# Convolution through band matrices, routing batch by batch with the sums on GpSimd, and experts chosen in two groups

## What is computed

```
z = layernorm(x)                                        # per token
top = 1 where the channel context is among the 76 largest of 128 positions, else 0
conv input, branch c (top) and s (1 - top): [max, mean] over the positions -> [B, 2, 512]
A = sigmoid(relu(batchnorm(conv1d(input, 2 channels, 7 taps))))       # one value per batch and channel
x = x + z * (top * A_c + (1 - top) * A_s)
f = layernorm(x)
p = softmax(f @ router_w.T + router_b)                  # 8 experts
w = the two largest p of a token, divided by their sum
x = x + 0.5 * sum over experts of w * (f @ A.T) @ Bm    # rank 16
```

## Time and profile before

| | |
|---|---|
| runs | 1105.84, 1101.44, 1104.09 us; median 1104.09 |
| the profiled execution | 1102.04 us, its span 1100.3 us |
| busy over the span | TensorE 999.7 us (91%), VectorE 706.1, ACT 515.7, GpSimd 469.3 |
| mean granted TensorE clock | 0.967 of full speed |

### The profile page before, as it was taken

The page is one execution under the profiler, slowest core; times in us unless marked ns, Lnnn a source line. Parts: engine busy times, 40 slices in busy tenths (PEclk is TensorE's granted clock), DMA queues, the critical chain, the costliest instruction groups (busy, mean ns, idle before and its releaser), DMA issues. The chain is left out here.

```text
span 1100.3 us, 18306 instructions
## 1 busy us (share of the span) xinstructions
PE 999.7 (91%) x6010; PEld 844.0 (77%) x6010; DVE 706.1 (64%) x1844; ACT 515.7 (47%) x1330; POOL 469.3 (43%) x362
## 2 busy tenths in 40 slices
PE   4999999999999999999999999999999999565465
PEld 3888888888888888888888888888878887333353
DVE  6566565656576767586555665665676575587384
ACT  3454444444444554445543543553555344167251
POOL 5554444444444545434444354353444352344200
PEclk9999999999999999999999999999999999799577
DMA  6433333323333323334232132222212220000002
GB/s 205 146 94 94 95 95 93 94 93 95 93 96 96 92 89 97 117 99 133 59 105 82 32 104 70 72 82 82 72 62 82 82 63 23 20 1 1 1 1 77
DMA packets 50412, 87.71 MB, mean 80 GB/s; under 512 B 6368, under 2 KB 15200, under 8 KB 50336
## 3 DMA queue, kind: packets, MB, share of 16 engines
q1 hardware_dynamic: 50336, 86.76, 25.5%
HBM read 84.64 MB, written 2.10 MB: 79 GB/s over the span
## 5 line engine op out<-in xcount | busy, mean ns | idle before, releaser
L540 POOL TENSOR_TENSOR wq_lo<-raw_q,wq_hi 128x512 fp32r<-128x512 f32 x64 | 82.8, 1293 | 263.6 <-DVE prob L1213 257.3
L1493 PE MATMUL pX<-wv_lo,cT_hi 128*128 128x256 f32 x512 | 149.3, 292 | 0.2 <-ACT q_sb L678 0.2
L1196 DVE TENSOR_TENSOR score<-pS,b_mask 128x512 f32<-128x512 f32 x64 | 44.2, 691 | 161.4 <-PE pS L1671 148.1
L802 ACT ACTIVATE prob<-score,neg_max 128x128 f32<-128x128 f32 x256 | 99.7, 391 | 97.2 <-DVE neg_max L1199 97.2
L1494 PE MATMUL pX<-wv_hi,cT_lo 128*128 128x256 f32 x512 | 144.0, 281 | 0.0
L1495 PE MATMUL pX<-wv_hi,cT_hi 128*128 128x256 f32 x512 | 144.0, 281 | 0.0
L540 POOL TENSOR_TENSOR wv_lo<-raw_v,wv_hi 128x1024 fp32r<-128x1024 f32 x32 | 77.6, 2425 | 124.9 <-ACT wv_hi L678 124.9
L678 ACT ACTIVATE v_sb<-pX 128x512 f32<-128x512 f32 x64 | 38.2, 597 | 163.2 <-PE pX L1495 163.2
L1493 PE MATMUL pX<-xT_lo,wq_hi 128*128 128x512 f32 x256 | 106.0, 414 | 6.1 <-POOL wq_lo L540 5.1
L1493 PE MATMUL oacc<-wo_lo,aT_hi 128*128 128x512 f32 x256 | 100.5, 393 | 5.1 <-DVE aT_lo L1191 3.8
L1493 PE MATMUL pX<-cT_lo,wk_hi 128*128 128x512 f32 x256 | 105.0, 410 | 0.0
(11 more groups left out here) (276 smaller groups left out, 2387.1 us busy)
## 6 DMA issues: line engine op xcount, KB each, us to landing
raw_k<-in_wk SPq DMA_DIRECT2D x64, 256.0 KB, 2.9
raw_q<-in_wq SPq DMA_DIRECT2D x64, 256.0 KB, 3.5
raw_v<-in_wv SPq DMA_DIRECT2D x32, 512.0 KB, 4.2
raw_o<-in_wo SPq DMA_DIRECT2D x64, 256.0 KB, 2.7
b_raw<-in_bias SPq DMA_DIRECT2D x64, 64.0 KB, 2.8
g_raw<-in_w_gate SPq DMA_DIRECT2D x16, 172.0 KB
g_raw<-in_w_up SPq DMA_DIRECT2D x16, 172.0 KB
f_raw<-in_w_down SPq DMA_DIRECT2D x4, 688.0 KB, 4.7
```

Source lines behind the costliest of these rows:

```text
L540: g.tensor_tensor(w_lo[c][:], w_raw[c][:], w_hi[c][:].bitcast(F32), ALU.subtract).then_inc(s_w_lo[c], 1)
L802: e = a.activation(prob[:, b, :], score[:, b, :], ACT.Exp, bias=neg_max[:, b:b + 1], accum_out=row_sum[:, b:b + 1])
L1196: v.tensor_tensor(score[:], pS[:].rearrange("p (b s) -> p b s", b=HB), b_mask[:], ALU.add).then_inc(s_scored, 1)
L1493: mm(dst, lh, rl, start=start, stop=False, skip_group_check=lint)
```

## The change

The taps are no longer multiplied into the statistics. In seven attention steps (20 to 23, 28 to 30) VectorE builds two band matrices of 128 x 384 from `diag` and the taps, and the convolution is three products for each of them. ACT scales the means as it sums. Scale and shift of batch norm go into the Tanh, and relu behind it; a one-element Exp follows the Tanh. The mean over the channels is taken out of `ra` once (at token tile 0 of the second half), so that the routed rows are transposed and multiplied without subtracting the mean, and the reciprocal deviation is put on as ACT copies `rh`. Routing goes batch by batch: VectorE makes product and statistics, GpSimd the sum and the power. The choice is made for batches 0 to 3 while 5 to 7 are still being routed, then for 4 to 7; it takes the largest of the logits rather than of the probabilities, and divides by the sum of the two chosen. The expert products of batches 0 to 3 stand between the routing of 5 to 7.

```diff
+CHOSEN = 2.0 ** 127
+        BAND_STEPS = (20, 21, 22, 23, 28, 29, 30)
+        l_bank = (pYb[:].bitcast(F32), pA[:, 512:1024])
...
@@ gpsimd, at the end @@
-            with pool.Fori(0, B // 2) as p:
-                rsqrt(rs1[:], ve1[:], p + HB + 6)
+            def routed_rstd(t):
+                pool.wait_ge(s_x3_var, t + 1)
+                g.tensor_tensor(rs3[:, t:t + 1], ve3[:, t:t + 1], neg_half[:, 0:1], ALU.pow).then_inc(s_x3_rstd, 1)
+            for t in range(B):
+                pool.wait_ge(s_zc, t + 1)
+                g.tensor_tensor(xr[:, t, :], zc[:, t % 2, :], xr[:, t, :], ALU.add).then_inc(s_x3, 1)
+                if t >= 1:
+                    routed_rstd(t - 1)
+            routed_rstd(B - 1)
@@ scalar, sums of the statistics @@
                             last = a.activation(sum_junk[:, br, lt, :], split[:, br, lt, :], ACT.Copy,
+                                                scale=1.0 / (CRUCIAL, REST)[br],
@@ scalar, behind the feed-forward layer @@
             act.wait_ge(s_zn, 1)
-            a.activation(cz[:], cz2[:], ACT.Tanh, scale=0.5).then_inc(s_sig, 1)
+            for br in range(2):
+                last = a.activation(cz2[:, :, br, :], cz[:, :, br, :], ACT.Tanh, scale=bn_scale[:, br:br + 1],
+                                    bias=bn_shift[:, 0:1])
+            last.then_inc(s_sig, 1)
+            a.activation(exp_again[:], ident[:, 0:1], ACT.Exp)
             act.wait_ge(s_dA, 1)
...
+            def routed_heads(t):
+                act.wait_ge(s_r_proj, t + 1)
+                act.wait_ge(s_x3_rstd, t + 1)
+                a.activation(rh[:, t, :], pA[:, 0:E + ER], ACT.Copy,
+                             scale=rs3[:, t:t + 1]).then_inc(s_rh, 1)
...
+            weights_of(1)
+            weights_of(2)
+            for t in range(B):
+                routed_out(t)
+                if t + 3 < B:
+                    weights_of(t + 3)
+                if t == HB:
+                    route_exp(0)
+                if t > HB:
+                    lora_out(t - HB - 1)
+                routed_heads(t)
+            lora_out(HB - 1)
+            route_exp(1)
+            for t in range(HB, B):
+                lora_out(t)
@@ vector, in attention, called in step behind early_end @@
+            def bands(n):
...
+                    for c in range(2):
+                        tap = taps[:, c * TAPS + j:c * TAPS + j + 1]
+                        if j == 0:
+                            v.tensor_scalar(band[c][:], diag[:, 0:3 * P], tap, None, ALU.mult)
+                        else:
+                            last = v.scalar_tensor_tensor(out=band[c][:], in0=diag[:, j:j + 3 * P], scalar=tap,
+                                                          in1=band[c][:], op0=ALU.mult, op1=ALU.add)
@@ vector, behind attention @@
             for t in range(HB + 2):
+                if t == 0:
+                    dve.wait_ge(s_ra_sum, 1)
+                    v.tensor_scalar(ra_mean[:, 0, :], ra_bank, 1.0 / D, None, ALU.mult)
+                    dve.drain()
+                    v.tensor_tensor(ra[:], ra[:], ra_mean[:].to_broadcast([P, KT, E + ER]),
+                                    ALU.subtract).then_inc(s_ra, 1)
                 ffn_step(t)
-            for j in range(TAPS):
-                v.tensor_scalar(tapped[:, j], stat[0][:], taps[:, j:j + 1], None, ALU.mult)
...
             dve.wait_ge(s_conv, 1)
-            v.tensor_copy(cz[:], conv)
...
             dve.wait_ge(s_rstd, HB + 6)
+            v.tensor_scalar(bn_scale[:], rs1[:], gb[:, 0:1], 0.5, ALU.mult, ALU.mult).then_inc(s_zn, 1)
+            dve.wait_ge(s_sig, 1)
+            v.tensor_scalar(cz[:], cz2[:], 0.0, 0.5, ALU.max, ALU.mult)
             dve.drain()
+            v.tensor_scalar(other[:], cz[:, :, 1, :], 0.5, None, ALU.add)
+            v.tensor_tensor(dA[:], cz[:, :, 0, :], cz[:, :, 1, :], ALU.subtract).then_inc(s_dA, 1)
...
+            def gated(t):
+                dve.wait_ge(s_c_trans, t + 1)
+                if t >= 2:
+                    dve.wait_ge(s_x3, t - 1)
+                v.tensor_tensor(zc[:, t % 2, :], c_bank[t % 2][:], z[:, t, :], ALU.mult).then_inc(s_zc, 1)
+            def routed_stats(t):
+                dve.wait_ge(s_x3, t + 1)
+                v.bn_stats(st3[:, t, :], xr[:, t, :])
...
+                v.tensor_scalar(ve3[:, t:t + 1], mv3[:, t, 1:2], EPS, None, ALU.add).then_inc(s_x3_var, 1)
+            def route(i):
+                group = slice(i * HB, (i + 1) * HB)
+                dve.wait_ge(s_rh, (i + 1) * HB)
+                v.tensor_tensor(prb[:, group, 0:E], rh[:, group, 0:E], rb[:].to_broadcast([P, HB, E]), ALU.add)
+                for t in range(i * HB, (i + 1) * HB):
+                    v.max(best[:, t, :], prb[:, t, :])
+                v.tensor_tensor(logit[:, group, :], prb[:, group, 0:E],
+                                best[:, group, 0:1].to_broadcast([P, HB, E]), ALU.subtract).then_inc(s_top_logit, 1)
+                for t in range(i * HB, (i + 1) * HB):
+                    v.match_replace(prw[:, t, :], best[:, t, :], prb[:, t, :], CHOSEN)
+                dve.wait_ge(s_r_exp, i + 1)
...
+            gated(0)
+            gated(1)
+            for t in range(HB):
+                routed_stats(t)
+                gated(t + 2)
+            routed_stats(4)
+            route(0)
+            for t in range(HB):
+                weighed(t)
+            gated(6)
+            routed_stats(5)
+            finished(0)
+            gated(7)
+            routed_stats(6)
+            finished(1)
+            routed_stats(7)
+            finished(2)
+            finished(3)
+            route(1)
+            for t in range(HB, B):
+                weighed(t)
+            for t in range(HB, B):
+                finished(t)
@@ tensor @@
             for t in range(-1, HB + 2):
                 ffn_step(t)
+                if t == -1:
+                    pe.wait_ge(s_const_in, 16 * 6)
+                    for kt in range(KT):
+                        last = mm(ra_bank, ones[:], ra[:, kt, :], start=kt == 0, stop=kt == KT - 1)
+                    last.then_inc(s_ra_sum, 1)
...
+            for c in range(2):
+                pe.wait_ge(ready[c][0], EARLY_Z)
+                pe.wait_ge(ready[c][1], B - EARLY_Z)
+                mm(pA[:, 0:KT * width], band[c][:, P:2 * P], stat[c][:], start=c == 0, stop=False,
+                   skip_group_check=True)
+                mm(pA[:, width:KT * width], band[c][:, 2 * P:3 * P], stat[c][:, 0:KT - 1], start=False, stop=False,
+                   skip_group_check=True)
+                last = mm(pA[:, 0:(KT - 1) * width], band[c][:, 0:P], stat[c][:, 1:KT], start=False, stop=c == 1,
+                          skip_group_check=True)
...
+            coef_transposes(0)
+            coef_transposes(1)
+            for t in range(HB):
+                routed_transposes(t)
+                coef_transposes(t + 2)
+                router(t)
+            routed_transposes(4)
+            coef_transposes(6)
+            router(4)
+            routed_transposes(5)
+            hidden_transpose(0)
+            router(5)
+            coef_transposes(7)
+            hidden_transpose(1)
+            lora(0)
+            routed_transposes(6)
+            router(6)
+            hidden_transpose(2)
+            lora(1)
+            routed_transposes(7)
+            hidden_transpose(3)
+            lora(2)
+            router(7)
+            lora(3)
...
```

More of the change, by code:

```diff
@@ L129, in layers_kernel @@
         e_down = sbuf("e_down", [P, D])
+        stat = [sbuf(f"stat{c}", [P, KT, 2, B]) for c in range(2)]
         att = ExitStack()
@@ L921, in _ @@
             act.wait_ge(s_zn, 1)
-            a.activation(cz[:], cz2[:], ACT.Tanh, scale=0.5).then_inc(s_sig, 1)
-            act.wait_ge(s_dA, 1)
[L925 to L930, removed]
-                        last = a.activation(coef[:, t, lt, :], top[:, t // HB, lt, t % HB, :], ACT.Identity,
-                                            scale=dA[:, lt, at(t)], bias=cz[:, lt, 1, at(t)])
-                    last.then_inc(s_coef, 1)
@@ new lines, in _, with weights_of, routed_out @@
+            last.then_inc(s_sig, 1)
+            a.activation(exp_again[:], ident[:, 0:1], ACT.Exp)
+            act.wait_ge(s_dA, 1)
+            def weights_of(t):
+                for lt in range(KT):
+                    last = a.activation(coef[:, t, lt, :], top[:, t // HB, lt, t % HB, :], ACT.Identity,
+                                        scale=dA[:, lt, t:t + 1], bias=other[:, lt, t:t + 1])
+                last.then_inc(s_coef, 1)
+            def routed_out(t):
+                act.wait_ge(s_f_t, t + 1)
+                if t >= 2:
+                    act.wait_ge(s_r_proj, t - 1)
+                copy(fT[:, t % 2, :], f_bank[:, t % 2 * 512:(t % 2 + 1) * 512]).then_inc(s_fT, 1)
@@ L1868, in _, with coef_transposes @@
[L1868 to L1871 removed]
+            def coef_transposes(t):
+                if t == 0:
```

(24 more changed lines are left out.)

247 lines of the change are left out of this document (85 added, 162 removed).

## The result

The changed kernel takes 1086.7 us (median of four runs, 1084.2 to 1087.9) against 1102.97 in runs beside it: a ratio of 0.9853, 95% interval 0.9829 to 0.9878, 16.3 us faster. Two executions on record stand far apart from the others of their kernel and are in none of the ratios here: 1124.38 us of the kernel before, beside the first experiments, and 2038.98 us of the kernel with one choice. The changed kernel's profiled execution took 1084.23 us with a span of 1082.5, that of before 1102.04 with 1100.3.

What follows compares the result with a forecast made beforehand. TensorE bounds the kernel to about 945 us, handovers between engines the last 70 us. 6.85 + 0.2 + 2.4 + 0.7 + 3.8 − 0.1 = 13.9 us gives execution 1088.1, or 1090.2 as median; it took 1089, range 1083 to 1095.

Steps and rivals of the forecast that it cites:

- Bands in attention: Two VectorE instructions in each of seven attention steps, mostly in idle time: cost 0.1 us, bounds 0 and 0.4.
- attention ends within 0.5 us of before: Sign that the prediction is right: the end of attention moves by no more than 0.5 us.
- Mean of the router weights: Four TensorE products and two VectorE instructions before token tile 0 of the second half: costed at nothing, 1 us if uncovered.
- Convolution: Six products instead of 13, first batch-norm reduction straight from PSUM at 1034.0: gain 6.85 us, bounds 6.0 and 7.3.
- Batch norm and gates: From the reduction to the gate difference: smaller scaling, two Tanh, two more small VectorE instructions: gain 0.2 us.
- Routing: Gate difference to last row: ACT bounds at 2.5 to 2.8 us a batch, first choice delays products 6, 7: gain 2.4.
- Second choice: Last row to first weighted product: four batches, no table load, but VectorE waits 1.9 for output tile 3: gain 0.7.
- End: First weighted product to the span's end: four tiles at half clock, 1.7 us each, 11.3 in all: gain 3.8.
- full-clock rival: TensorE's clock stays high to the end or rises sooner, last four tiles take 0.97 each: gain 17.5, 1085.5; chance 0.2.
- contention: GpSimd and VectorE hold each other up in routing: 3 to 5 us, so 1092 to 1094; chance 0.16, late clock included.
- the batches don't overlap: Routing queues stand behind GpSimd's sum; wholly serial 7.1 us a batch, 12 us slower than before, 1115; chance 0.04.
- the clock never rises: All routing rows at half clock, 4.2 us of TensorE a batch, so the time is 1103; chance 0.05.

Runs made afterwards that it cites:

- the first experiments: The earliest follow-up runs, which the text doesn't single out; the kernel before had medians of 1102.3 to 1102.6 us beside the experiments.
- the kernel with one choice: Changed kernel with one choice of all eight batches behind the last row, all eight output tiles behind it: 1087.2 us.
- with it alone: Kernel before with only the new convolution (band matrices, means scaled on ScalarE, six products): 1097.4 us, ratio 0.9954.
- the filler: Changed kernel plus 20 unread bf16 products on TensorE behind output tile 3, while it waits for the second choice: 1085.0 us.
- the kernel with one choice and filler at the gates too: Changed kernel with one choice of all eight batches, unread TensorE products during it, ahead of the convolution, between batch-norm sums and during gates: 1083.2 us.
- that without the gate filler: Changed kernel with one choice of all eight batches and 21 unread TensorE products while it is made: 1082.9 us.
- no early Exp: Changed kernel without the one-element Exp behind Tanh, so the first choice loads the Exp table: 1090.7 us.
- the kernel without the hole: Changed kernel with product 6 and statistics 5 inside the first choice, output tile 3 finished behind the second choice's weighed products: 1085.3 us.
- the kernel with sums on VectorE: Changed kernel with the eight routing sums on VectorE behind each product, GpSimd keeping only the powers: 1089.2 us.
- the one with filler at the gates: Changed kernel plus unread TensorE products ahead of the convolution (10), between batch-norm sums (2) and during the gates (9): 1085.7 us.

## Why the prediction was right

It said 1089.0, range 1083 to 1095, 13.9 us gained in the span. It was 16.24 in the tail; the median of 1086.7 lies in the range. Of the gain 2.3 us were missed: the pace of the routing and the end were both costed too dear, by 2.8 together, and three small misses the other way come to 0.5.

- *Bands in attention*, costed 0.1: measured 0.2 to 0.3, of the seven steps. The sign "attention ends within 0.5 us of before" failed (1.25 sooner), but it could tell nothing of the bands, since that mark differs by more between executions. *Mean of the router weights*, costed at nothing: its subtraction took 1.20, and still ended ahead of SiLU's product; from attention's residual to the last split it is 82.8 before and 82.5 after.
- *Convolution*, 6.85: measured 6.78, and 6.70 with it alone. The sequence predicted is what the timeline shows.
- *Batch norm and gates*, 0.2: measured 0.03. The two Tanh take 0.72 together where 0.56 was taken.
- *Routing*, 2.4: measured 3.73. The mechanism was right (ScalarE sets the pace, a hole of 4 us before product 6), and the size off: "2.5 to 2.8 us a batch" should have been 2.31. The durations 0.60, 1.64 and 0.36 of neighbouring ScalarE instructions overlap by about 0.1 each; from start to start they are 0.50, 1.53 and 0.28. Adding durations and a handover for each overstated the busy engine's queue. The end of row 3 came 0.85 sooner behind dA than laid out (15.85 for 16.7), and the hole and what follows it gave another 0.4 (VectorE was held for 4.10 us, 1053.78 to 1057.88, for 4.5).
- *Second choice*, 0.7: measured 0.41; VectorE did wait for output tile 3, for 2.37 behind row 7 where 1.9 was taken.
- *End*, 3.8: measured 5.29. "Four tiles at half clock" held for one tile and part of the next; then the clock rose. Before, it had stayed low for two tiles and part of the third. From the first weighed product to the first tile's matmul it was 1.14, not 0.9. The full-clock rival stood 3.6 below the forecast, of which its own terms (four tiles at 0.97 for 1.7, two transposes at half their 0.2) give 3.1; 1.5 came by itself (9.77 for 11.3), and the filler brought another 1.46.

The mechanisms were right in each part. What the sum didn't show is which part of the routing and choice earns the gain. The one-choice kernel does: the new routing 8.5 (hardly for the clock: before, the sums of the last three pairs start 6.49 apart, at 1056.90, 1063.39 and 1069.88, with the clock low for the first and up for the second), the table load behind Tanh and the new choice 1.5, the two groups about nothing. They are neither good nor bad in themselves; they hold products 6 and 7 for as long as they hide tiles.

The rivals: contention is refuted (684 against 694 ns); "the batches don't overlap" and "the clock never rises" did not occur (rows 2.31 apart; 1.00 from 1046 to 1072); "the clock stays high to the end" was half true, for two of four tiles.

Attention's end differs by up to 4 us between executions, the largest disturbance in these medians (the kernel with one choice and filler at the gates too has a tail 2.1 shorter than that without the gate filler, and the same median). The traces show where most of it lies: in the granted clock, at two places. From the last score addition to the residual it takes 12.1 us in seven profiles, with the clock at 1.00, but 13.5 in four and 15.1 in one (no early Exp), in which the clock is at 0.50 for part of attention's last products. And in four profiles the clock falls at 724 to 726, behind an idle stretch of 1.95 us that the others have too, and that step takes 1.2 us longer. Busy time by stretch, the kernel with one choice, then the changed kernel, in the same output products:

```profile
944.00:946.00 2.00, 1.88 (x5) 1.50 (x6) 0.08 (x2) 0.00 (x0) 0.00 (x0) 0.50 0.00 0
...
942.00:944.00 2.00, 2.00 (x10) 1.63 (x10) 0.00 (x0) 0.00 (x0) 0.00 (x0) 1.00 0.00 0
```

Left open: why the clock falls there in some executions and not in others, with the same instructions.

## What to carry to other kernels

In a tail of small handovers, an idle stretch on TensorE costs twice: once as a wait, and again in the products behind it if the clock falls. A choice that was 1.4 us later went with a loss of 3.1. So before work is split into groups to hide the last stage, lay out which queue the first group's work stands in: here it delayed about as much as it hid, and moving a product and a statistic inside it and one output tile behind the other was worth 3.4 us in the profiled tails (1.4 of it in the last four tiles, where the clock stayed up; the medians show 1.4 in all and can't tell that much). And for a busy engine, take intervals from start to start in the timeline, not sums of durations.

## What the hardware showed that was not expected

The length of the idle stretch alone doesn't tell whether the clock falls. TensorE idle for 3.27 us before the last tiles left it at 1.00 (the kernel without the hole), idle for 4.09 us it went to 0.50 (changed kernel). But idle for 3.02 us in the kernel before (from 1071.58 on) it fell too, to 0.68 and then 0.50 in the 2 us stretches from 1074 on, and so it did behind 2.49 us in the first choice of the kernel with sums on VectorE. In attention, around 722, the same 1.95 us of idling left it at 1.00 in eight profiles and at 0.50 in four. So a hole of this size is a risk, and a single profile with the clock up is no proof that an order of work keeps it up. Its rise took, in the same sequence of four tiles, one and a half tiles in the changed kernel and two and a half in the one with filler at the gates, 1.1 us more with the same instructions, for a cause that these traces don't show. And behind bf16 products of 512 columns that had raised it, the convolution's products of 48 and 64 columns and the small sums (TensorE busy 1.36 of the 2 us from 1032 on) did not keep it: it stood at 0.50 from 1034 on.
